# Local attention: where the turned probabilities lie in PSUM, and the order of turn, context and scores

## The reference, cut to what matters

```
q, k, v = split(x @ w_qkv.T + b_qkv)              # 16 heads of 16
scores  = q . k_window / sqrt(16)                  # 33 keys around each token
attn    = softmax(scores)
ctx     = attn . v_window
x       = x + ctx @ w_out.T + b_out
```

## Time and profile before

| | us |
|---|---|
| median of 3 runs | 1601.63 (1600.05 to 1602.63) |
| the profiled execution | 1593.04 |
| its span | 1591.2 |
| PE busy | 1565.0 (98%) |
| DVE busy | 1203.1 (76%) |
| ACT busy | 967.7 (61%) |
| POOL busy | 738.9 (46%) |
| local attention, from the first scores to the last context | 1265 to 1468 |

### The profile page before, as it was taken

One profiled execution on the slowest core, in us unless ns is written; L12 is line 12 of the kernel. 1 busy time (PEld: TensorE's weight loads), 2 busy tenths in 40 slices (PEclk: granted clock), 3 DMA queues, 4 the chain that ended last, 5 costly groups with the idle time before them and its releaser, 6 DMA issues.

```text
span 1591.2 us, 46573 instructions
## 1 busy us (share of the span) xinstructions
PE 1565.0 (98%) x17333; PEld 1141.6 (72%) x17334; DVE 1203.1 (76%) x2543; ACT 967.7 (61%) x1816; POOL 738.9 (46%) x690
## 2 busy tenths in 40 slices
PE   8999999999999999999999999999999999998999
PEld 4665559999666776766655669999666777777676
DVE  7777777888676766768776667887788878888876
ACT  5454545777477767764433336777476677675765
POOL 3442242444246566552332333444245577886343
PEclk9999999999999999999999999999999999999999
DMA  8132223433311211003210123333433022221001
GB/s 266 60 106 92 88 91 102 120 118 119 96 32 27 40 26 26 1 1 104 80 54 27 40 80 102 119 119 110 103 67 53 2 82 76 69 63 43 28 26 53
DMA packets 91468, 115.81 MB, mean 73 GB/s; under 512 B 9456, under 2 KB 76688, under 8 KB 91344
## 3 DMA queue, kind: packets, MB, share of 16 engines
q1 hardware_dynamic: 70992, 71.21, 15.5%
q0 software_dynamic: 20352, 42.88, 9.5%
HBM read 66.14 MB, written 47.90 MB: 72 GB/s over the span
## 4 chain that ended last, share of the span: by engine, by line
PE 87%; DVE 6%; ACT 2%; issue 2%; DMA 1%; POOL 1%; SPq 1%; DVEq 0%; ACTq 0%; POOLq 0%
PE ps L2156 20%; PE ps L2158 20%; PE ps L2157 20%; PE ps L2391 3%; PE ps L2441 3%; PE ps L2442 3%; PE ps L2392 3%; PE ps L2172 2%; PE ps L2724 2%; PE ps L2355 2%; PE ps L2685 2%; PE ps L2699 2%; PE ps L2543 1%; PE ps L2503 1%; PE ps L2568 1%
## 5 line engine op out<-in xcount | busy, mean ns | idle before, releaser
L818 POOL DMA_INDIRECT routed<-work x142 | 139.4, 982 | 210.1 <-ACT work L1103 205.5
L2156 PE MATMUL ps<-xt_hi,wsh 128*128 128x512 f16 x508 | 192.6, 379 | 3.2 <-DVE work L1640 2.4
L2158 PE MATMUL ps<-xt_hi,wsh 128*128 128x512 f16 x508 | 192.5, 379 | 0.0
L2157 PE MATMUL ps<-xt_lo,wsh 128*128 128x512 f16 x508 | 192.5, 379 | 0.0
L1034 ACT ACTIVATE work<-ps 128x512 f32<-128x512 f32 x128 | 76.2, 597 | 165.0 <-PE ps L2158 164.7
L1640 DVE SCALAR_TENSOR_TENSOR work<-ps,work 128x512 f32<-128x512 f32 x128 | 88.1, 690 | 74.7 <-ACT work L1034 72.2
L2156 PE MATMUL ps<-wsh,work 128*128 128x256 f16 x512 | 139.5, 273 | 0.7 <-DVE work L1569 0.6
L2158 PE MATMUL ps<-wsh,work 128*128 128x256 f16 x512 | 139.5, 273 | 0.0
L2157 PE MATMUL ps<-wsh,work 128*128 128x256 f16 x512 | 139.5, 273 | 0.0
L1130 ACT ACTIVATE work<-ps,cols 128x512 f32<-128x512 f32 x120 | 82.8, 691 | 54.9 <-PE ps L2392 43.8
L2441 PE MATMUL ps<-w2q,work 128*128 128x256 f16 x512 | 113.4, 273 | 0.0
(11 more groups left out here) (299 smaller groups left out, 5067.3 us busy)
## 6 DMA issues: line engine op xcount, KB each, us to landing
work<-expert_x SPq DMA_DIRECT2D x142, 129.0 KB, 2.1
later<-values SPq DMA_DIRECT2D x32, 256.0 KB, 3.5
yg<-in_w_later SPq DMA_DIRECT2D x9, 498.0 KB
w1q<-in_w_later SPq DMA_DIRECT2D x9, 498.0 KB, 3.8
yg<-in_w SPq DMA_DIRECT2D x16, 256.0 KB, 3.5
values<-wsh SPq DMA_DIRECT2D x8, 512.0 KB, 2.9
expert_x<-work SPq DMA_DIRECT2D x30, 129.0 KB, 3.5
yg<-routed SPq DMA_DIRECT2D x7, 512.0 KB, 3.7
```

What stands on the lines that cost most here:

```text
L818: nc.gpsimd.indirect_dma_start(routed[:, :], bass.IndirectOffsetOnAxis(m.homes[:, i:i + 1], 0), m.t_y[:, i % 4, :], None).then_inc(s[f"til ...
L2156: nc.tensor.matmul(out_, a[0], b[0], start=start, stop=False)
L2157: nc.tensor.matmul(out_, a[0], b[1], start=False, stop=False)
L2158: return nc.tensor.matmul(out_, a[1], b[0], start=False, stop=stop)
```

## The change: what it does

`turn_bank` is gone. `turn_place` puts the eight turned blocks of a quarter, two to a bank, into the second halves (columns 256 to 511) of the banks 2 to 5 that hold the scores; `turned_half` is what ACT reads: two half banks at a time. The last sequences keep banks 5 and 6. `turn` is no longer split.

```diff
-        def turn_bank(g, t, b):
-            return 6 if turned_amid(g, t) else WTURN + b
+        def turn_place(g, t, j):
+            if turned_amid(g, t):
+                return ps[:, WSCORE + j // 2, BPT * KB + j % 2 * P:BPT * KB + (j % 2 + 1) * P]
+            return ps[:, WTURN + j // 4, (j % 4) * P:(j % 4 + 1) * P]
+
+        def turned_half(g, t, b):
+            if turned_amid(g, t):
+                return ps[:, WSCORE + 2 * b:WSCORE + 2 * b + 2, BPT * KB:BPT * KB + 2 * P]
+            return ps[:, WTURN + b:WTURN + b + 1, :]
...
 (ACT, step)
+                    turned(g - 1, 2)
                     queries_keys(g + 1, 1 - u, (0,))
                     ct_hi(g - 1, 1 - u, 1)
-                    turned(g - 1, 2, (0,))
                     exps(g, 0)
-                    turned(g - 1, 2, (1,))
                     queries_keys(g + 1, 1 - u, (1,))
 
+                    turned(g - 1, 3)
                     queries_keys(g + 1, 1 - u, (KT,))
                     ct_hi(g - 1, 1 - u, 2)
-                    turned(g - 1, 3, (0,))
                     exps(g, 1)
                     queries_keys(g + 1, 1 - u, (KT + 1,))
-                    turned(g - 1, 3, (1,))
-
+
+                    turned(g, 0)
+                    values_rows(g + 1, (0,))
                     xt_hi_of(g + N0(n) + 2, u, WSCORE)
-                    values_rows(g + 1, (0,))
                     ct_hi(g - 1, 1 - u, 3)
-                    turned(g, 0, (0,))
                     exps(g, 2)
                     values_rows(g + 1, (1,))
-                    turned(g, 0, (1,))
-
+
+                    turned(g, 1)
                     if not second_last(g):
                         normed_rows(g + 1)
                     ct_hi(g, u, 0)
-                    turned(g, 1)
                     exps(g, 3)
...
 (PE, scores)
-                    if is_second(g) and t == 1:
-                        pe.wait_ge(s["pt_copied"], 4)
+                    if wide(g, t):
+                        pe.wait_ge(s["pt_copied"], 2 * (g * TPS + t - 2))
+                    elif is_last(g) and t == 1:
+                        pe.wait_ge(s["pt_copied"], 2 * (g * TPS + t - 3))
...
+                def turn(g, t):
+                    pe.wait_ge(s["norm_ready"], g * TPS + t + 1)
+                    if has_turn(g, t, 1):
+                        pe.wait_ge(s["pt_copied"], (g * TPS + t) * 2)
+                    else:
+                        pe.wait_ge(S[n - 1]["y_taken"], 2 * NSEQ + 2)
+                    if turned_amid(g, t):
+                        pe.wait_ge(s["windowed"], g * TPS + t + 3)
+                    for j in range(BPT * KT):
+                        ins = nc.tensor.transpose(turn_place(g, t, j), m.p[t][:, 2 * j:2 * j + 2].rearrange("p a b -> p (a b)"), ident)
+                        if j % 4 == 3:
+                            ins.then_inc(s["pt_ready"], 1)
...
 (PE, step)
                         if t == 2:
-                            pe.wait_ge(s["windowed"], g * TPS + t + 1)
+                            turn(g2, t2)
+                            rows_part(g, u, t, 0)
+                            pe.wait_ge(s["pt_copied"], (g * TPS + t) * 2 - 3)
                             transposes(g + N0(n) + 2, b=WSCORE)
-                        rows_part(g, u, t, 0)
-                        context(*turns_back(g, u, t, 3))
-                        if t != 2:
-                            scores_next(g, u, t)
-                        turn(g2, t2, (0,))
-                        rows_part(g, u, t, 1)
-                        turn(g2, t2, (1,))
-                        if t == 2:
+                            context(*turns_back(g, u, t, 3))
+                            rows_part(g, u, t, 1)
                             xt_ready(g + N0(n) + 2)
                             scores_next(g, u, t)
+                        else:
+                            rows_part(g, u, t, 0)
+                            turn(g2, t2)
+                            context(*turns_back(g, u, t, 3))
+                            scores_next(g, u, t)
+                            rows_part(g, u, t, 1)
```

More of the change, by code:

```diff
@@ L1290, in turned @@
                         act.wait_ge(s["pt_ready"], (g * TPS + t) * 2 + b + 1)
-                        nc.scalar.activation(m.pt[:, t % 2, 4 * b:4 * b + 4].rearrange("p a b -> p (a b)"),
-                                             ps[:, turn_bank(g, t, b), :], ACT.Copy).then_inc(s["pt_copied"], 1)
+                        own = turned_half(g, t, b)
+                        nc.scalar.activation(m.pt[:, t % 2, 4 * b:4 * b + 4].rearrange("p (c d) b -> p c (d b)", c=own.shape[1]),
+                                             own, ACT.Copy).then_inc(s["pt_copied"], 1)
                 def ct_hi(g, u, t):
```

## The result

| | before | after |
|---|---|---|
| median of 7 runs | 1601.42 us | 1605.91 us |
| lowest to highest | 1599.68 to 1602.63 | 1603.96 to 1608.51 |
| ratio, 95% interval | | 1.0026 (1.0015 to 1.0037) |
| profiled execution, its span | 1593.04, 1591.2 | 1604.57, 1602.7 |

The changed kernel is slower by 4.5 us, 0.26%. The two spans differ by 11.5 us, and most of that is not the change: in the two profiled executions the context of (0,0) starts at 1291.50 and 1298.54 us, and nothing of the change lies before that. So I compare three stretches inside local attention, each from one instruction to another: the entry, from the context of (0,0) to DVE's window step on scores(1,2); five periods, from there to the window step on scores(6,2), which the prediction calls w; and the exit, from there to the last context. What follows the last context took 124.4 us in both.

The account below looks back on a forecast made before the run. PE was taken to bound the kernel. Entry +0.2, five periods +3.5 and exit -0.85 sum to +2.8 us, 1595.9 for the profiled execution; with 8.6 us for the timed runs, 1604.4, range 1598.5 to 1609.

Parts of the forecast that it names:

- What bounds the kernel: Local attention: PE is the bound, ACT has slack, DVE 3.9 us of slack per sequence; the last sequence is DVE-bound.
- The lost switch: Each slot on PE: eight turns at once instead of four twice, 5.56 us against 5.61, about 1 us in all.
- Wait (1): Scores wait until ACT has copied the same slot's turn; cost zero, with 0.3 to 0.4 us to spare.
- Wait (2): Slot 2: PE's turn waits 0.1 us for DVE's window step, and scores(g,3) another 0.1 us for xt_lo.
- Wait (3): Slot 3: the turn of (g,1) waits for DVE's window step on scores(g,3), 0.7 us a sequence.
- The issue time stays: PE's 0.93 us of issue time per sequence was taken to stay, giving 0.7 us a sequence, +3.5 over five periods.
- rival A: Slot 3's new wait lets PE's instruction stream catch up and the 0.93 us issue time goes; 1600.1 us, chance 0.20.
- The entry: Sequence 1: +0.2 us; the turn of (0,2) waits for DVE where PE stood about as long in issue.
- The exit: Last sequence, bound by DVE: its chain starts 0.85 us earlier, as the exponentials no longer wait behind a split turn.
- Rival B: Exponentials reach DVE's sum of (g,2) over 0.14 us late, lengthening PE's wait; 1607.4 us at half a microsecond, chance 0.25.
- rival C: Slot 3's wait doesn't appear and part of the issue time goes with the switches; -4 us, 1597.6, chance 0.10.

Follow-up runs that it names:

- Taking its cause away on DVE's side: Against the changed kernel, DVE reads scores of (g,3) with its window step before summing the exponentials of (g,2), sequences 1 to 6; ratio 1.0016 to the kernel before.
- the late copies: Against the changed kernel, ACT's query copy in slot 0 and key copy in slot 1 stand ahead of the turn's copies again; ratio 1.0043 to the kernel before.
- The kernel with the forty waits: Against the changed kernel, 40 waits on a count reached long ago put on PE ahead of local attention; ratio 1.0042 to the kernel before.
- The changed kernel's second profile: The changed kernel run again as it is, in the job with the forty waits; ratio 1.0028 to the kernel before.
- the turn came late in slot 3: Against the changed kernel, PE's slot 3 of sequences 1 to 5 runs projection half, context, turn, projection half, scores; ratio 1.0048 to the kernel before.
- the scores stood last: Against the kernel before, an ACT swap in sequence 6 and scores at the end of slots 0 and 3 (slot 3 not in 6); ratio 1.0066.
- the last kernel: Against the kernel before, an ACT swap in sequence 6 and the last sequence's last normalization on POOL ahead of its bias sum, not DVE; ratio 0.9989.

## Why the prediction was right, and where it was off

The time came out at 1605.9 for 1604.4, in the range, and just on the other side of the 3.2 us that I called no change; I gave "same" 0.48 and "slower" 0.39, so by my own line the less likely of the two came.

1. *What bounds the kernel*: right. PE is the bound up to sequence 6, DVE behind it.
2. *The lost switch, 5.56 for 5.61 us a slot*: right. From the context of slot 3 to that of slot 0 the changed kernel takes 5.58 us (1350.07 to 1355.65), from there to that of slot 1 5.56, and eight turns behind products take 0.96 up to the context (1354.69 to 1355.65).
3. *Wait (1), scores on ACT's copies, at no cost*: right in the five periods, with the cover measured at 0.2 to 0.3 us. (The 0.62 us in its sum, from the turn to the first copy, has no row in the prediction, which reads 0.69; the changed kernel has 0.63, 1354.69 to 1355.32.) In sequence 1 the norming of the rows (2.08 us) stood ahead of the copies on ACT, and PE waited 0.18.
4. *Wait (2), slot 2's two small waits*: right; scores(g,3) at w + 7.12 for w + 7.05.
5. *Wait (3), slot 3, 0.7 us*: right, to the step of DVE. w + 8.66 for 8.65, w + 9.97 for 9.90; PE stands 0.52 us by the rows, which show idle time from the end of the last product, or 0.68 over the 0.11 us after which a turn follows products (1322.52 to 1323.31). Taking its cause away on DVE's side, and nothing else, brought the turn 0.54 us forward and the period down by 0.80. The prediction looked for the wait in sequences 2 to 6; it is there in 1 to 6.
6. *The issue time stays (forecast) or goes (rival A)*: it stayed, 0.84 us a period over the reckoned 24.08, for 24.24 - 23.4 = 0.84 in the kernel before. That the two agree to 0.1 us is in part luck, since the issue time varies by 0.3 us a period from one profile to the next. The sum behind it is not: with each of a sequence's 624 matmuls at the median of its five distances from start to start, which leaves the stalls out, the period is 23.38 us before (reckoned 23.4) and 24.09 after (24.08). Rival A fell for this wait. Its mechanism seems to exist: the wait made in slot 0 by the late copies, 0.58 us, lengthened the period by only 0.14 to 0.19.
7. *The entry, +0.2*: mis-sized; it is +1.43. I let the waits of slot 0 cover the issue stall of 0.94 us that stood there before. They did not: 0.28 + 0.41 + 0.18 us of waits came, and 0.69 + 0.27 of issue stood as well. The kernel with the forty waits shows that the stalls make the difference: with the same kind of waits (0.42 + 0.41 + 0.20 us) and no stall the entry is 13.52 us, 0.14 over the 13.38 before.
8. *The exit, -0.85*: mis-sized; it is -0.36. The chain did start 0.66 us earlier for the 0.85 reckoned, but a small DVE instruction that had taken 0.10 us now fell under POOL's work and took 0.67; the last normalization gave 0.26 of that back.

Terms 7 and 8 are 1.2 and 0.5 us, both to the slow side, and they are the whole difference between +2.8 and +4.5. The changed kernel's second profile has an entry of 15.38, so the first of them is 1.2 to 1.8. Rival B (exponentials late by more than 0.14 us) and rival C did not occur.

## What to carry to other kernels

When a stage moves ahead in an order written by hand, ask of each wait that moves with it how long the awaited engine's queue is from the last point at which the two met; here DVE's rows of the old trace, added up, gave the new wait to 0.1 us. Here the wait was better taken away by reordering the awaited engine than by moving dense work of the bounding engine, whose issue stalls grew when it was moved. And compare inner stretches of the traces, not spans: here the profiled executions differed by up to 8 us ahead of all that was changed.

## What the runs showed of the hardware

Nearly all of PE's issue stalls stand at fixed places of the instruction stream, at multiples of 252 matmuls and weight loads from each other, and move when instructions are put ahead of them. They cost from nothing to 2.2 us each. They were longest in the two kernels in which PE's order was changed once more: up to 1.8 us where the turn came late in slot 3, 2.2 us where the scores stood last.

A small DVE instruction with two inputs in SBUF took longer beside POOL. The shift of 128x4 elements took 0.10 us with POOL idle and 0.67 under its subtraction (POOL's from 1453.56 to 1455.46, DVE's from 1454.80 to 1455.47 in the changed kernel), ending when POOL did. The normalization of 128x1024 took 3.02 to 3.32 us on DVE, beside POOL's bias sums, where DVE's window step of the same size, with one input in PSUM, takes 1.2. The Trainium skill, "SBUF — State Buffer", section "Who interferes with whom", says that a DVE instruction with two SBUF inputs contends with a GpSimd instruction that reads SBUF; the rows of the shift agree. For the normalization no run has DVE do it with POOL idle, so how much of its 3 us is owed to POOL is not shown. But POOL was held up beside it: its four bias sums of 128x256 took 3.78 us in the changed kernel, the first under DVE's normalization, and 2.79 in the last kernel, where POOL does that tile itself in 1.91 us, ahead of its bias sums.

```profile
1472.12 3.02 DVE L2039 TENSOR_TENSOR work<-work 128x1024 f32<-128x1024 f32 x1
1474.02 3.78 POOL L760 TENSOR_TENSOR x<-x,rows 128x256 f32<-128x256 f32 x4
...
1467.19 2.79 POOL L753 TENSOR_TENSOR x<-x,rows 128x256 f32<-128x256 f32 x4
```

(The last row is from the kernel with the last norm on POOL.)
